# A four-layer block on one core: the linear part of the scan layer moved into PSUM accumulation, its order cut to five steps, and the attention's value matmuls spread over four column groups

## The reference, cut to what matters

```python
# 1. causal attention: 16 heads of width 8, rope on q and k
scores = einsum('bhqd,bhkd->bhqk', q, k) * SCALE + add_mask
out = einsum('bhqk,bhkd->bhqd', softmax(scores), v)      # then @ Wo.T + bo
# 2. ffn: 8 experts, the 2 best of a token, and one expert shared by all (hidden width 512)
scores = sigmoid(xf @ Wg.T + bg + bias); top_scores, top_idx = top_k(scores, 2)
# 3. scan layer (ED = 256 channels, N = 16 states)
proj = einsum('bld,ed->ble', x, W_in); x_conv, x_ssm = split(proj, 2)
x_conv = depthwise_conv3(x_conv, conv_w)                  # taps at l-1, l, l+1
dtv = mean(x_ssm, -1)[..., None] * W_dt[:, 0]
a = einsum('ble,en->bln', dtv, A); u = einsum('ble,en->bln', dtv * x_ssm, Bm)
m_t = a_t * m_{t-1} + u_t                                 # scan over 512 tokens
y = einsum('bln,ne->ble', m_seq, Cm) + Dv * x_ssm
gate = sigmoid(y); z = x_conv * gate + y * (1 - gate)
layer = einsum('ble,de->bld', z, W_out) + x               # the layer's own residual
# 4. the ffn of layer 2 again, same weights
```

## Time and profile before

| | before |
|---|---|
| median of three runs | 732.47 us (729.3 to 733.21) |
| profiled execution | 739.22 us |
| its span, first to last instruction | 737.3 us |
| busy share of the span: PE, DVE, ACT, POOL | 70%, 67%, 46%, 37% |
| mean granted TensorE clock | 0.847 of full speed |

### The profile page before, as it was taken

How to read it: one execution, slowest core, us unless ns; L and a number is a source line. 1 busy time by engine, 2 the same in 40 slices (tenths; PEclk the granted TensorE clock), 3 DMA queues, 4 the chain that set the end, 5 groups by cost and what they waited for, 6 DMA issues and landing times.

```text
span 737.3 us, 14795 instructions
## 1 busy us (share of the span) xinstructions
PE 515.5 (70%) x5290; PEld 345.0 (47%) x5290; DVE 494.5 (67%) x1405; ACT 342.2 (46%) x462; POOL 269.8 (37%) x291
## 2 busy tenths in 40 slices
PE   2487888788888875655579889156777666688860
PEld 1454545445454444433367668113352444577750
DVE  5778786776867743565637677366979676487664
ACT  1245645665566552443527577013243434376550
POOL 5019007402900001675415456312334255156550
PEclk9789999999999996767769899666586877799995
DMA  8999200000210001000146673300000000775715
GB/s 275 328 334 335 83 1 2 2 1 1 86 46 1 2 1 32 28 16 26 33 133 205 190 213 101 104 28 0 14 16 23 7 30 26 209 201 168 218 53 172
DMA packets 58782, 69.05 MB, mean 94 GB/s; under 512 B 6653, under 2 KB 46070, under 8 KB 58454
## 3 DMA queue, kind: packets, MB, share of 16 engines
q1 hardware_dynamic: 54166, 58.72, 26.5%
q0 software_dynamic: 4544, 9.38, 3.8%
HBM read 37.20 MB, written 30.88 MB: 92 GB/s over the span
## 4 chain that ended last, share of the span: by engine, by line
another core or an unknown queue 20%; PE 19%; DVE 5%; issue 4%; DMA 3%; ACT 1%; SPq 1%; POOL 0%; POOLq 0%; DVEq 0%
PE ps L1223 7%; PE ps L1237 4%; PE ps L1238 3%; PE ps L1217 2%; DMA arena<-y_dram 2%; DVE x_all L1707 2%; PE ps L1211 1%; PE ps L1188 1%; PE ps L1268 1%; DMA y_dram<-arena,goes_to 1%; SPq L502 1%; DMA qk_sb<-rows_dram 1%; ACT arena L860 0%; DVE arena L1650 0%
## 5 line engine op out<-in xcount | busy, mean ns | idle before, releaser
L1416 DVE TENSOR_REDUCE row_maxima<-ps 128x2 f32<-128x256 f32 (+3 forms) x128 | 99.0, 817 | 43.0 <-PE ps L987 42.8
L694 POOL DMA_INDIRECT y_dram<-arena,goes_to x78 | 89.1, 1143 | 97.0 <-DVE goes_to L1678 85.6
L739 ACT ACTIVATE probs<-ps 128x768 f32<-128x768 f32 (+1 forms) x96 | 82.5, 884 | 81.2 <-PE ps L1012 81.2
L555 POOL TENSOR_TENSOR rstd<-var_eps,minus_half 128x4 f32<-128x4 f32 x16 | 17.0, 1065 | 223.0 <-DVE var_eps L1353 223.0
L860 ACT ACTIVATE arena<-ps,up_back 128x512 f32<-128x512 f32 x78 | 53.2, 682 | 75.8 <-PE ps L1223 54.9
L686 POOL DMA_INDIRECT rows_dram<-probs,idx x64 | 67.6, 1056 | 54.0 <-DVE idx L1614 34.1
L1032 PE MATMUL ps<-probs,v_tok 128*16 128x256 f32 (+3 forms) x512 | 74.7, 434 | 2.5 <-ACT probs L739 2.5
L1237 PE MATMUL ps<-w,probs 128*128 x312 | 62.6, 281 | 18.3 <-issue 12.3
L1223 PE MATMUL ps<-arena 128*128 128x128 f16 x936 | 69.8, 228 | 2.6 <-DVE arena L1673 2.3
L1223 PEld LDWEIGHTS ps<-arena 128*128 128x128 f16 x936 | 62.7, 103 | 15.9 <-issue 9.3
L1684 DVE SCALAR_TENSOR_TENSOR probs<-arena,hid_scale,probs 128x512 f16<-128x512 f32 x78 | 58.3, 747 | 8.5 <-ACT probs L865 7.0
(11 more groups left out here) (237 smaller groups left out, 1106.9 us busy)
## 6 DMA issues: line engine op xcount, KB each, us to landing
arena<-weights_dram SPq DMA_DIRECT2D x78, 256.0 KB
rows_dram<-grids SPq DMA_DIRECT2D x2, 8840.0 KB, 43.7
qk_sb<-rows_dram SPq DMA_DIRECT2D x78, 65.0 KB
arena<-in_w SPq DMA_DIRECT2D x2, 2304.0 KB
arena<-y_dram SPq DMA_DIRECT2D x8, 512.0 KB, 3.6
weights_dram<-w SPq DMA_DIRECT2D x2, 1152.0 KB, 7.5
y_dram<-arena,goes_to POOLq DMA_INDIRECT x78
x_all<-in_x SPq DMA_DIRECT2D x4, 256.0 KB, 8.6
```

The lines of the kernel that those rows point to most:

```text
L694: nc.gpsimd.indirect_dma_start(y_dram.ap(), bass.IndirectOffsetOnAxis(ap=goes_to[:, n % YT:n % YT + 1], axis=0), y_t[:, n % YT, :], None). ...
L739: nc.scalar.activation(probs[:, n % 2, :, PROB_AT[u]:PROB_AT[u] + size], ps[:, of:of + 2, 0:size], ACT.Exp).then_inc(slot_free[slot_of(("T ...
L1416: ins = nc.vector.tensor_reduce(row_maxima[:, t, 2 * p:2 * p + 2], ps[:, of:of + 2, o:o + keys], AX.X, ALU.max)
```

## The change

1. `weigh_values`: the key blocks are shared out between two halves, (0, 3) and (1, 2), 640 queries each. Half and head choose the column group, so one pair uses all four groups of 32 columns. An even pair's values stand in the first 16 columns of the 32 that are loaded, an odd pair's in the last 16, zeros beside them (`v_tok` is laid out anew, 41 words for a pair of pairs and head), so that both pairs of a quad add up in the same bank.
2. `weighed_T`: the two halves are partial sums. A product with a constant matrix `fold` (128 x 64) transposes and adds them, where four transposes stood.
3. Scan layer: everything linear becomes accumulation in PSUM from `xsT`. `y` is `win_dv` times x plus `cm` times the state. `d` = convolution less `y` is three products with `taps` (the convolution's taps multiplied into `win`, with `win_dv` taken from the middle one), two of them on 511 shifted columns, plus `cm_less` (= -`cm`) times the state. ScalarE reads `y` from PSUM for the gate, DVE computes `z = d * gate` in one instruction. What `y` and the residual give to the output is a product with a matrix `direct` (128 x 128, identity added) and one with `direct_state` (16 x 128), made once. `scan_conv`, `scan_y`, the copies `scan_projected` and GpSimd's residual add are gone.
4. `scan_matrices` (DVE, after `place` of the first router's batch 0), `scan_products` (TensorE) and `scan_direct` (DVE) make these matrices on the chip.
5. The scan layer and second router run in five steps: batch `i-1` is finished and routed in the step in which batch `i` is started. `tokens_split` now stands behind `choose`, `scan_outputs(i)` ahead of `ranks(i-1)`.
6. Five late loads are issued when GpSimd's last rope is done (`roped`), `b1e` and `cmT` as before after the last projection (`last_in`). `fold` is loaded with the attention's constants. `mean`, `var_eps` and `rstd` have two halves.

The diff, cut to its core:

```diff
+HALVES = ((0, 3), (1, 2))
-    for i in range(B + 2):
-        if 1 <= i <= B:
-            order += [("y", i - 1, 0), ("y", i - 1, 1)]
+    for i in range(B + 1):
+        if i >= 1:
+            order += [("mo", i - 1)]
         if i < B:
             order += [("sx", i)]
-        if i >= 2:
-            order += [("gr", 1, i - 2)]
+        if i >= 1:
+            order += [("gx", 1, i - 1)]
         if i < B:
-            order += [("dt", i), ("xs", i, 0), ("xs", i, 1), ("xc", i, 0), ("xc", i, 1)]
...
+            order += [("dt", i)]
+        if i >= 1:
+            order += [("gg", 1, i - 1)]
+        if i < B:
+            order += [("y", i, 0), ("y", i, 1), ("d", i, 0), ("d", i, 1)]
+        if i >= 1:
+            order += [("gr", 1, i - 1)] + of_shared(1, i - 1)
+            order += [("rt", 1, i - 1), ("sd", 1, i - 1), ("ba", 1, i - 1)]
...
# SP
+            sp.wait_ge(roped, B)
+            for dst, src in ((win, win_in), (win_rows, win_rows_in), (wout, wout_in), (taps, conv_rows_in), (win_dv, dv_rows_in)):
+                sp.dma_start(dst, src).then_inc(late_in, 16)
             sp.wait_ge(slot_free[slot_of(("wo", B - 1))], filled(("wo", B - 1)))
...
# GpSimd
-            nc.gpsimd.memset(v_tok[:], 0.0).then_inc(pads_set, 1)
+            nc.gpsimd.memset(v_flat[:], 0.0).then_inc(pads_set, 1)
...
-                    nc.gpsimd.tensor_tensor(x_all[:, i], x_all[:, i], xsf[:, i % 2], ALU.add).then_inc(residual_ready, 1)
...
# ScalarE
+                    nc.scalar.activation(gate[:, c, :], ps[:, of, :], ACT.Sigmoid).then_inc(bank_free[of], 1)
...
# TensorE, weigh_values
+                for j in range(TT):
+                    half = 0 if j in HALVES[0] else 1
+                    for h in range(2):
+                        group = OW * (2 * half + h)
+                        at_v = (((a % 2) * TT + j) * HP + p // 2 * 2 + h) * VS + VW * (p % 2)
+                        mm = pe.matmul(ps[group:group + OW, PV_BANK, j * P:L],
+                                       v_flat[:, at_v:at_v + OW],
+                                       probs[:, n % 2, h, at[j]:at[j] + L - P * j],
+                                       start=(p % 2 == 0 and j == HALVES[half][0]), stop=(j == HALVES[half][1]), skip_group_check=True)
...
# TensorE, weighed_T
-                    mm = pe.transpose(ps[:, to, t * P:(t + 1) * P], weighed[:, t * P:(t + 1) * P], ident[:])
+                    mm = pe.matmul(ps[:, to, t * Q * VW:(t + 1) * Q * VW], weighed[:, t * P:(t + 1) * P], fold[:], start=True, stop=True)
...
# TensorE, scan_outputs (before the state: 2 + 6 products; behind it: 4)
+                x = xsT[:, b % 2, :]
+                for c in range(2):
+                    to = give2(("y", b, c))
+                    pe.matmul(ps[:, to, :], win_dv[:, c * P:(c + 1) * P], x, start=True, stop=False, skip_group_check=True)
+                for c in range(2):
+                    to = give2(("d", b, c))
+                    of = slice(c * P, (c + 1) * P)
+                    pe.matmul(ps[:, to, :], taps[:, 1, of], x, start=True, stop=False, skip_group_check=True)
+                    pe.matmul(ps[:, to, 1:L], taps[:, 0, of], x[:, 0:L - 1], start=False, stop=False, skip_group_check=True)
+                    pe.matmul(ps[:, to, 0:L - 1], taps[:, 2, of], x[:, 1:L], start=False, stop=False, skip_group_check=True)
+                pe.wait_ge(state_ready, b + 1)
+                pe.wait_ge(direct_ready, 1)
+                for name, matrix in (("y", cm), ("d", cm_less)):
+                    for c in range(2):
+                        mm = pe.matmul(ps[:, bank_of((name, b, c)), :], matrix[:, c * P:(c + 1) * P], state[:, b % 2, :], start=False,
+                                       stop=True, skip_group_check=True)
+                        full((name, b, c), mm)
...
# TensorE, scan_project_back: ahead of the 8 products with z
+                for t in range(TT):
+                    tokens, result = slice(t * P, (t + 1) * P), ps[:, to, t * D:(t + 1) * D]
+                    pe.matmul(result, xsT[:, b % 2, tokens], direct, start=(t == 0), stop=False, skip_group_check=True)
+                    pe.matmul(result, state[:, b % 2, tokens], direct_state, start=False, stop=False, skip_group_check=True)
...
# VectorE, scan_z and scan_matrices
+                    dve.wait_ge(bank_free[bank_of(("y", b, c))], count_of(("y", b, c)))
+                    of = take2(("d", b, c))
+                    nc.vector.tensor_tensor(z[:, c, :], ps[:, of, :], gate[:, c, :], ALU.mult).then_inc(bank_free[of], 1)
...
+                dve.wait_ge(late_in, 16 * 5)
+                nc.vector.tensor_scalar(cm_less, cm[:], -1.0, None, ALU.mult).then_inc(direct_ready, 1)
+                nc.vector.tensor_tensor(taps, taps, win[:, 0:ED].unsqueeze(1).broadcast_to([P, K, ED]), ALU.mult)
+                post_link(nc.vector.tensor_tensor(win_dv, win_dv, win[:, ED:2 * ED], ALU.mult))
+                nc.vector.tensor_tensor(taps[:, 1], taps[:, 1], win_dv, ALU.subtract)
+                for c in range(2):
+                    ins = nc.vector.tensor_scalar(dv_rows[:, c, :], win_rows[:, c, :], dv[:, c:c + 1], None, ALU.mult)
...
# VectorE, the order of the steps
+            for i in range(B + 1):
                 if i < B:
                     combine(0, i)
                     norm_stats(x_all[:, i], post_link)
+                if i >= 1:
+                    scan_add(i - 1)
+                    norm_stats(x_all[:, i - 1], post_link, X_SCALE)
                 if i < B:
                     scan_apply(i)
+                if i >= 1:
+                    tokens(1, i - 1)
                 if i < B:
                     scan_steps(i)
+                if i >= 1:
+                    choose(1, i - 1)
+                    tokens_split(1, i - 1)
+                if i < B:
+                    scan_z(i)
+                if i >= 1:
+                    place(1, i - 1)
+                    if i == B:
+                        map_tiles(1)
+                    shared_low(1, i - 1)
+                    shared_add(1, i - 1)
```

More of the change, by code:

```diff
@@ L316, in part @@
             return (flat if dt == F32 else flat.bitcast(dt)).rearrange(f"p ({names}) -> p {names}", **sizes)
+        tile_row, weight_row, tile_expert = (weighed[:, NT * i:NT * (i + 1)].bitcast(I32) for i in range(4, 7))
+        which = part(weighed, 7 * NT, [NT, C], BF16)
+        expert_of, tiles_past, first_row, list_end = (weighed[:, NT * i:NT * (i + 1)] for i in range(4))
         probs_words = probs[:].rearrange("p a b c -> p (a b c)")
@@ L756, in pre_values @@
                 of = take(("v", a))
-                nc.scalar.copy(v_tok[:, a % 2, :, :, 0:HD],
-                               ps[:, of, :].rearrange("p (t h d) -> p t h d", t=TT, h=H)).then_inc(slot_free[slot_of(("v", a))], 1)
+                for q in range(2):
+                    ins = nc.scalar.copy(v_tok[:, a % 2, :, :, 2 * VW * q:2 * VW * q + HD].rearrange("p t (g h) d -> p (t g) h d", h=2),
+                                         ps[:, of, :].rearrange("p (g q h d) -> p q g h d", q=2, h=2, d=HD)[:, q])
+                ins.then_inc(slot_free[slot_of(("v", a))], 1)
             def pre_keys(a, half):
@@ L1260, in scan_project @@
                 read2(("wa",))
-                pe.wait_ge(late_in, 64)
                 read2(("sw",))
@@ L1264, in scan_project @@
                 full(("dt", b), mm)
-                for name, k in (("xs", 2), ("xc", 0)):
-                    for c in range(2):
-                        to = give2((name, b, c))
-                        mm = pe.matmul(ps[:, to, :], win[:, (k + c) * P:(k + c + 1) * P], xsT[:, b % 2, :], start=True, stop=True)
-                        full((name, b, c), mm)
             def scan_outputs(b):
-                pe.wait_ge(state_ready, b + 1)
+                x = xsT[:, b % 2, :]
                 for c in range(2):
@@ new lines, in scan_matrices @@
+            def scan_matrices():
+                dve.wait_ge(late_in, 16 * 5)
[3 more added lines that the diff above has]
+                nc.vector.tensor_tensor(taps[:, 1], taps[:, 1], win_dv, ALU.subtract)
+                for c in range(2):
+                    ins = nc.vector.tensor_scalar(dv_rows[:, c, :], win_rows[:, c, :], dv[:, c:c + 1], None, ALU.mult)
+                ins.then_inc(products_ready, 1)
@@ L1784, in _ @@
                     place(0, i - 1)
+                if i == 1:
+                    scan_matrices()
+                if i == 3:
+                    scan_direct()
                 if i == B:
@@ L1854, in shape_constants @@
         "grids": grids, "counts": np.stack([later, np.ones((P, P))], 1).astype(mybir.dt.np(BF16)),
-        "cos": table(cos), "sin": table(sin), "ident": np.eye(P, dtype=np.float32),
+        "cos": table(cos), "sin": table(sin),
+        "fold": np.tile(np.eye(Q * VW, dtype=np.float32).reshape(2, 2, VW, Q * VW).transpose(1, 0, 2, 3).reshape(Q * VW, Q * VW), (2, 1)),
+        "ident": np.eye(P, dtype=np.float32),
```

252 lines of the change are left out of this document (93 added, 159 removed).

## The result

| | before | after |
|---|---|---|
| median of the runs, us | 731.5 (4 runs) | 741.4 (3 runs), ratio 1.0134, 95% interval 1.0076 to 1.0191 |
| the same again on another chip | 731.39 (28 runs) | 740.96 (6 runs), ratio 1.0156, 1.0106 to 1.0205 |
| span of the profiled execution | 737.3 | 741.2 |
| mean granted TensorE clock | 0.847 | 0.829 |

The forecast was 713 in a range of 697 to 730. A fourth run of the kernel after took 2574 us and is left out of the median and the ratio. The ratios are given with their intervals as they were recorded; the quotient of two medians can differ from them by some 0.3%.

What follows compares the result with a forecast made beforehand. TensorE was taken to lead the attention and DVE the scan stage, whose full steps pass to TensorE's chain. Attention -21, late loads -1.7, start +0.5, scan +3.3 sum to -18.9: 732.47 to 713.6 us, range 697 to 730.

Steps and rivals of the forecast that it cites:

- Part 1: Attention: value blocks over four column groups save 25.1 us, the fold gives back 4.0; -21 us together.
- (a): Value blocks: the four groups do not run together, block stays 2.33 us; 738.6 us, slower; chance 0.13.
- (b): Value blocks: queue looks past only one blocked pass, block takes 1.6 us, attention gives 12; 722 us; chance 0.12.
- pairs beside the rope: Attention: 8 of 31 periods, where DVE has 0.9 us free; a saving of 0.4 us each.
- Parts 2 to 4: Longer memset at the start +0.5 us; late loads issued earlier -1.7; making the matrices in the first router hidden, 0.
- early loads: First router's start: five loads issued at the rope's end save 1.7 of a 4.00 us wait.
- Part 5, "Steps": Scan stage: five steps of 21.7, three times 36 and 31.8 us, 161.5 against 158.2; +3.3 us.
- The short passes: Scan stage: 16 short TensorE passes added for a batch, priced at 2 us.
- (d): Scan stage: TensorE at half clock or longer shared-result waits, 3 us more in four steps, +12; 725 us; chance 0.08.
- (c): Scan stage gains 15 us as TensorE's work fills idle time, steps about 32 us; 698 us or so; chance 0.12.

Runs made afterwards that it cites:

- warm2: att_only plus unread filler products on TensorE at places where its profile showed TensorE waiting; ratio to the kernel before 0.9874, attention 218.0 us.
- att_only: Kernel before with only the attention's part (four-group value blocks, fold, new v_tok), scan stage as before; ratio to before 0.9961.
- att_c: att_only again on another chip; ratio to the kernel before 0.9929, attention 217.8 us.
- after_c: The kernel after, unchanged, again on another chip; 740.96 us, ratio to the kernel before 1.0156.
- six_y_old_pv: Kernel after with six scan steps, y added by DVE, residual by GpSimd, and the attention's old value blocks, transposes and v_tok; ratio to before 1.0059.
- six_y_warm: Kernel after with six scan steps, y added by DVE, residual by GpSimd, and TensorE fillers in five attention pairs; ratio to before 0.9942.
- scan_only: Kernel after with the value blocks, transposes and v_tok of the kernel before; ratio to before 1.0268, scan stage 173.3 us.

## Why the prediction was wrong

*Part 1, the block: right.* Four groups run together, 1.28 us a block, and rivals (a) and (b) are out. The clock was not in the sum: I let every period shrink and left the clock at 0.99. In six periods of the kernel after (from blocks 4, 7, 15, 19, 20 and 30) it fell more than in the same periods of some other profile, and they are 1.4, 1.2, 1.2, 1.8, 1.2 and 1.4 us longer than there, 8.2 together. This is an estimate and an upper one: no profile without fillers had all of them at the higher clock, it fell elsewhere instead, and the attention with the new blocks and the fold took 217.0 to 220.6 us in all of these (213.2 with fillers). The fold took 1.08 and not 0.90, 16 x 0.18 = 2.9. These two are 11.1 of the 12.0 us that lack (9.1 for 21.1). In part of the pairs beside the rope, worth 0.4 each in the sum, nothing came: the periods from blocks 2 and 3 are 0.1 shorter and 0.7 longer than before, at a clock of 1.00 and 0.99.

*Part 1, what it brings to the whole* is less than its stage on some chips: 9 to 12 us shorter in the profile gave 0.987 in warm2 but 0.996 and 0.993 in att_only. The tile loops went from 81 to 83 us in warm2 with the clock there from 0.94 to 0.91. I can't show where the rest goes on the two chips of att_only and att_c, since no profile of the kernel before was taken on them. The second tile loop is a candidate: on one chip it took 93.4 us at clock 0.88 in att_c and 86.7 to 88.5 at 0.93 to 0.95 in after_c, six_y_old_pv and six_y_warm. Whether the kernel before has 93 there too is not known.

*Parts 2 to 4* were small and stayed small; the 1.7 us of the early loads did not come.

*Part 5, "Steps", is the step that failed:* the stage was to grow by 3.3 us. By the table's lengths it grew by 20 to 21, and by 16 in the repeat, a miss of 12 to 18 us. That is the larger part of the distance between a kernel 18.9 us faster and one 10 slower; the attention's missing 12.0 (10 in the repeat) is the other. By steps the forecast was 21.7, 36, 36, 36 and 31.8, measured are 21.5, 46.2, 37.6, 36.5 and 35.0.

I took a full step as a sum of pieces at the mean prices of the stage before and gave all three 36 us. Three terms of it were wrong. The passes ahead of `ranks`: I put in 12, which is what the change adds; all 24 of `scan_outputs` stand there and took 14.4, 12.7 and 10.7 us instead of 7.8. The short passes: 5.7 us in step 1 and 3.4 in step 2 instead of 2. The clock: I used mean prices, and step 1 ran at 0.67, with the first 6 of its 24 passes at 0.94 and `shared_up` at 4.9 us for 2.75 in the next steps. The same step at 0.86 took 39.1 us (scan_only). That steps 2 and 3 came close to 36 all the same is in part luck: something else in the sum was priced too high by about as much, and I have not worked out what.

The order of the steps is not what the sum missed, since 36 us was a step in the new order. It is what makes the design a loss: with the same products and the same 132.2 us of busy TensorE, six steps took 164.2 us and five 173.3, all of it waiting. I never summed the new products in the old order. What the clock adds to this, 10 us in the first profile of the kernel after and 4 in the repeat, is not fixed by the order alone, as scan_only shows; why it fell there is open.

I had counted the half clock only in rival (d), at 12 us and a chance of 0.08; step 1 is (d)'s mechanism, in one step and not in four. (c), the stage gaining from DVE's relief, got nothing beyond 158.0 to 164.2 us for 160 to 161, in six steps, and a longer stage in five.

## What to carry to other kernels

A loop that is shortened by one step takes away overlap: before counting the step saved, write down what the engine with the most work can do while the new step's first results are made; if nearly all of it belongs to the same chain, the step gets longer by what it waits (9 us of 173 here). Count everything that stands in the queue ahead of an instruction, not only what the change adds. Relief for the busiest engine is worth only the time for which it really leads, and work moved to TensorE has to be priced at the clock that its waits will leave it. When a change has two parts, time them apart: here the good one hid in the sum.

## What the runs showed of the hardware

- Products in different groups of 32 columns start together past a blocked one: four passes within 0.02 us, both passes of a later product of 384 columns ahead of the second pass of an earlier one of 512, 16 passes of 5120 columns in 1.28 us. The Trainium skill ("TensorE: Matmul & The Clock Gate", Part 3, What overlaps and what doesn't) has starts in strict queue order; the measurement decides against it for this form.
- Taking work from TensorE lowered its clock: 0.98 to 0.99 in the attention before, 0.91 to 0.94 after. Fillers in its waits brought 0.96 and 0.97.
- The same instructions met the two levels of the clock at different places from run to run: the scan stage's 612 passes and more kept TensorE busy 142.4 us in one execution and 132.2 in another.
- Eight float32 passes of 64 columns take 1.08 us, as long as eight of 128 columns: halving the columns saved nothing.
- The same kernel took 712 to 738 us on five chips (medians). In its four profiles, of 712 to 739 us, attention and scan stage are alike within 1 us; the tile loops (81 against 88 to 94 us each) and the first router (96 against 103) make the difference.
